# Level 32 of a blockwise triangular inverse: pairs of 32x32 tiles in different row and column groups of TensorE

## The reference

```python
def step(state, inp):
    q_t, k_t, v_t, b_t, g_t = inp
    state = state * jnp.exp(g_t)[..., None, None]
    for j in range(nh):
        kj = k_t[:, j]
        corr = jnp.einsum('bhk,bhkv->bhv', kj, state)
        u = (v_t[:, j] - corr) * b_t[:, j][..., None]
        state = state + jnp.einsum('bhk,bhv->bhkv', kj, u)
    o_t = jnp.einsum('bhk,bhkv->bhv', q_t, state)
    return (state, o_t)
```

## Time and profile before

| | us |
|---|---|
| median of 3 runs | 1023.55 |
| runs | 1021.53, 1023.55, 1026.05 |
| profiled execution, its own time | 1018.88 |
| its span | 1016.9 |
| PE busy | 884.0 |
| DVE, ACT, POOL busy | 526.5, 388.9, 335.1 |
| mean granted clock of TensorE | 0.93 of 2.4 GHz |

### The profile page before, as it was taken

How to read it: one execution, slowest core, us unless ns; L and a number is a source line. 1 busy time by engine, 2 the same in 40 slices (tenths; PEclk the granted TensorE clock), 3 DMA queues, 4 the chain that set the end, 5 groups by cost and what they waited for, 6 DMA issues and landing times.

```text
span 1016.9 us, 15663 instructions
## 1 busy us (share of the span) xinstructions
PE 884.0 (87%) x5306; PEld 629.4 (62%) x5307; DVE 526.5 (52%) x1233; ACT 388.9 (38%) x834; POOL 335.1 (33%) x648
## 2 busy tenths in 40 slices
PE   6586889999999999999999984871699999999993
PEld 3334466686766766766766874661466666666662
DVE  1377756867868768768778641345541111111113
ACT  2453746446456445545554420202222222222220
POOL 0105853547358357346454471000041000000005
PEclk9797979999999999999999995975599999999997
DMA  7303013102120130031021011009717100000104
GB/s 208 104 0 68 2 20 74 22 12 63 22 50 25 22 73 15 8 74 22 2 43 21 12 26 26 1 1 328 247 52 273 55 31 31 31 31 31 31 16 124
DMA packets 100623, 58.39 MB, mean 57 GB/s; under 512 B 62088, under 2 KB 95952, under 8 KB 100560
## 3 DMA queue, kind: packets, MB, share of 16 engines
q1 hardware_dynamic: 99024, 53.38, 19.4%
q0 software_dynamic: 1536, 4.20, 1.4%
HBM read 43.00 MB, written 14.55 MB: 57 GB/s over the span
## 4 chain that ended last, share of the span: by engine, by line
PE 71%; DVE 8%; ACT 5%; POOL 5%; issue 5%; DMA 4%; SPq 1%; ACTq 0%; DVEq 0%; POOLq 0%
PE bank L1480 15%; PE bank L524 10%; PE bank L1526 8%; PE bank L605 3%; PE bank L673 3%; DVE y L934 3%; PE bank L650 3%; PE bank L532 3%; POOL inv L1225 2%; POOL term L1222 2%; PE bank L635 2%; PE bank L581 2%; PE bank L654 2%; PE bank L649 2%; PE bank L1511 2%
## 5 line engine op out<-in xcount | busy, mean ns | idle before, releaser
L934 DVE SCALAR_TENSOR_TENSOR y<-bank,cwh,y 128x510 f32<-128x510 f32 (+2 forms) x240 | 177.6, 744 | 68.4 <-ACT y L745 64.6
L524 PE MATMUL bank<-xnT,wbuf 128*128 128x512 f32 x320 | 162.0, 631 | 7.5 <-DVE y L934 7.0
L1480 PE MATMUL bank<-f_wgu,f_xgT 128*128 x368 | 118.8, 466 | 0.0
L1222 POOL TENSOR_TENSOR term<-inv,blk 128x126 f32<-128x126 f32 (+22 forms) x248 | 87.4, 353 | 57.8 <-DMA blk<-a_blocks 39.0
L1734 DVE TENSOR_TENSOR f_act<-f_sg,bank 128x352 f32<-128x352 f32 x62 | 32.2, 521 | 142.0 <-PE bank L1480 140.0
L524 PEld LDWEIGHTS bank<-xnT,wbuf 128*128 128x128 f32 x320 | 56.2, 195 | 69.6 <-issue 53.4
L1225 POOL TENSOR_TENSOR inv<-inv,term 128x126 f32<-128x126 f32 (+22 forms) x248 | 91.2, 368 | 19.4
L1526 PE MATMUL bank<-f_wdn,f_actT 128*128 (+1 forms) x372 | 91.5, 387 | 0.8 <-ACT f_actT L1596 0.8
L1805 POOL DMA_INDIRECT f_back<-slots_y,f_slot x16 | 15.4, 960 | 228.1 <-DMA slots_y<-f_yb 221.5
L1583 ACT ACTIVATE f_sg<-bank 128x352 f32<-128x352 f32 x62 | 28.8, 464 | 160.8 <-PE bank L1480 160.8
L1480 PEld LDWEIGHTS bank<-f_wgu,f_xgT 128*128 128x128 f32 x368 | 66.2, 190 | 36.8 <-issue 7.6
(11 more groups left out here) (211 smaller groups left out, 1604.7 us busy)
## 6 DMA issues: line engine op xcount, KB each, us to landing
f_wgu<-in_exp_gu SPq DMA_DIRECT2D x8, 1408.0 KB, 8.9
f_wdn<-in_exp_dn SPq DMA_DIRECT2D x8, 640.0 KB, 9.7
blk<-a_blocks SPq DMA_DIRECT2D x16, 256.0 KB, 3.8
slots_x<-oT SPq DMA_DIRECT2D x24, 128.0 KB, 1.8
f_xg<-slots_x SPq DMA_DIRECT2D x24, 128.0 KB, 2.0
slots_y<-f_yb SPq DMA_DIRECT2D x23, 128.0 KB, 1.7
wbuf<-in_Wk SPq DMA_DIRECT2D x16, 128.0 KB, 3.6
wbuf<-in_Wv SPq DMA_DIRECT2D x16, 128.0 KB, 3.5
```

The lines of the kernel that those rows point to most:

```text
L524: last = mm(bankA[p % 2][:, :], wbuf[A.par][:, kt, wblk, :], xnT[:, kt, (p % 2) * 512:(p % 2 + 1) * 512], start=kt == 0, stop=kt == 1)
L934: v.scalar_tensor_tensor(out=y[p % 2][:, :, k:], in0=src[:, :, 0:SEQ - k], scalar=cwh[A.par][:, cb, 3 - k:4 - k], in1=y[p % 2][:, :, k:], ...
L1222: g.tensor_tensor(step_term, inv[:, 0:r, j:j + 1].to_broadcast([P, r, k]), blk[:, j:j + 1, j + 1:].to_broadcast([P, r, k]), ALU.mult).then ...
L1480: last = mm(gu[c][:, 0:FFH], xt[:, k, :], wgu[:, e, k, at:at + FFH], start=k == 0, stop=k == 1)
```

## The change

Each matmul of p32 and of t32 becomes two of 32x32, one for each pair of blocks (g = 0, 1). For p32 the weights are the 32x32 block of A in rows 0 to 31 (g = 0) or 64 to 95 (g = 1), and the result goes to partitions 32 to 63 or 96 to 127; for t32 the rows are 32 to 63 or 96 to 127 and the result goes to partitions 0 to 31 or 64 to 95. The row group of the array follows from the operands' partitions, the column group from the result's, so the two of a pair use different row groups and different column groups. Both write the same bank. The matmuls are issued in the order chunk 0 g 0, chunk 0 g 1, chunk 1 g 0, and so on. X1 needs only 32 columns, nothing has to be zero any more, the memsets and their semaphore go, and the copies read packed columns.

```diff
-    X1 = sb("X1", [P, BC, STEPS])
+    X1 = sb("X1", [P, BC, NB])
@@ tensor_program, item
                 if kind == "p32":
-                    last = mm(bank[:, cols], a_m, X1[:, m, :], start=True, stop=True)
+                    for g in range(2):
+                        src, out = slice(2 * g * NB, (2 * g + 1) * NB), slice((2 * g + 1) * NB, (2 * g + 2) * NB)
+                        last = mm(bank[out, k * NB:(k + 1) * NB], a_m[src, out], X1[src, m, :], start=True, stop=True)
                 elif kind == "t32":
-                    last = mm(bank[0:32, cols], P32[:, m, :], t_m.rearrange("p (g s c) -> p g s c", s=2, c=32)[:, :, 1, :], start=True, stop=True)
+                    for g in range(2):
+                        src, out = slice((2 * g + 1) * NB, (2 * g + 2) * NB), slice(2 * g * NB, (2 * g + 1) * NB)
+                        last = mm(bank[out, k * NB:(k + 1) * NB], P32[src, m, :], t_m[src, src], start=True, stop=True)
@@ scalar_program, item
+            tiles32 = bank[:, 0:BC // 2 * NB].rearrange("p (m c) -> p m c", c=NB)
             if kind == "p32":
-                if B.h == 0:
-                    act.wait_ge(zeros_done, 1)
-                a(P32[32:64, ms, :], full[32:64, :, 0:32], ACT.Copy)
-                a(P32[96:128, ms, :], full[96:128, :, 32:64], ACT.Copy).then_inc(p32_done, 1)
+                a(P32[32:64, ms, :], tiles32[32:64, :, :], ACT.Copy)
+                a(P32[96:128, ms, :], tiles32[96:128, :, :], ACT.Copy).then_inc(p32_done, 1)
             elif kind == "t32":
-                a(tt[0:32, ms, 32:64], full[0:32, :, 0:32], ACT.Copy)
-                a(tt[64:96, ms, 96:128], full[0:32, :, 32:64], ACT.Copy).then_inc(t32_done, 1)
+                a(tt[0:32, ms, 32:64], tiles32[0:32, :, :], ACT.Copy)
+                a(tt[64:96, ms, 96:128], tiles32[64:96, :, :], ACT.Copy).then_inc(t32_done, 1)
@@ vector_program, turn_blocks
-            if B.h == 0:
-                dve.wait_ge(zeros_done, 1)
-            else:
+            if B.h:
                 item_done(dve, "p32", B.h - 1, 1)
...
-                v.transpose(X1[rows_, :, g * NB:(g + 1) * NB], tt[rows_, :, rows_]).then_inc(x1_done, 1)
+                v.transpose(X1[rows_, :, :], tt[rows_, :, rows_]).then_inc(x1_done, 1)
@@ gpsimd_program
-        g.memset(X1[:, :, :], 0.0)
-        g.memset(P32[:, :, :], 0.0).then_inc(zeros_done, 1)
```

More of the change, by code:

```diff
@@ L303, in attention @@
     tt_zero = sem("tt_zero")
-    zeros_done = sem("zeros_done")
     a_out = sem("a_out")
```

## The result

| | kernel before | changed kernel |
|---|---|---|
| median | 1023.92 us (4 runs) | 997.67 us (4 runs) |
| runs | 1021.53 to 1026.05 | 991.33 to 1000.65 |
| profiled execution | 1018.88, span 1016.9 | 998.55, span 996.6 |
| PE busy | 884.0 | 858.3 |

The ratio is 0.9736, 95% interval 0.9684 to 0.9789. Two later series of the same kernel gave 0.9771 (0.9722 to 0.9820) and 0.9741 (0.9704 to 0.9778). The change is worth 2.3 to 2.7%, 24 to 27 us, where 11 were forecast. The predicted range of 996 to 1022 holds the median, but by its mechanism this is rival 1, and the forecast's own range, 1008 to 1018, was missed. The profiled execution of before, 1018.88 us, is not among the four and was faster than each of them.

The account below looks back on a forecast made before the run. It took TensorE (PE), 87% busy, to bound the kernel. Savings of 8.5 us in the six steady heads and 2.6 in heads 0 and 7, 11.1 in all, off the median 1023.55 gave 1012 us, range 996 to 1022.

Parts of the forecast that it names:

- rival 1: p32 and t32: the two tiles overlap fully, 14.5 ns a pass, 3.27 us saved a steady head, total 999; 25%.
- What bounds the kernel: Whole kernel: PE, busy 87% of the span, carries 71% of the last chain, so p32's saving arrives at the end.
- The price of a pass: p32 and t32 in 32x32 tiles: 29 ns a pass, 64 passes each, net 1.41 us saved per steady head (1 to 6).
- the low end: p32 and t32: 14.5 ns a pass, half of L498's 29, if the tiles overlap as fully and nothing else binds.
- the prediction's own sign: p32 and t32: the forecast is wrong if passes are not at 25 to 33 ns, whatever the total says.
- The 0.20 us for changes of shape: Around p32 in each steady head: one gap of about 0.10 us ahead and one behind.
- Heads 0 and 7: p32 and t32 at half clock: 58 ns a pass, clock rising at the same moment, together 2.6 us saved.
- What is late next: Behind the shorter p32: L649 needs U, smallest margin 0.7 us in head 1; nothing changes on X1's way.
- Rival 2: p32 and t32: passes of long runs come no closer than 56 ns, total 1040; decides from 40 ns on; 10%.
- rival 3: p32 and t32: the two row groups take turns in one bank, 0.10 us each change of tile, total 1062; 4%.
- Rival 4: Each head: PE arrives earlier and waits, 1.4 us of new waits, no change, 1021 to 1025; 10%.
- Rival 5: Steady heads: the clock falls since little of the array works, about 4.5 us lost in each, total 1040; 3%.

Follow-up runs that it names:

- full2: The changed kernel run again unaltered, with a later profile: 994.62 us for 1023.17 of the kernel before (0.9741).
- micro: Changed kernel with nine series of 32 small matmuls ahead of its work, one execution: 32.0 ns a pass for one 32x32 tile, 16.0 for two.
- grouped: Changed kernel with all eight chunks of g = 0 issued first, then all of g = 1: 1020.62 us, 0.9954 of the kernel before.
- again: The changed kernel run once more unaltered: 1001.82 us for 1026.69 of the kernel before (0.9771).
- mixed2: Changed kernel with t32 of heads 0 and 7 as one matmul per chunk, as before: 992.80 us against 994.62 for the changed kernel unaltered.
- warm2: Changed kernel with 8 and 18 full matmuls on old data while PE waits for X1 in heads 0 and 7: 990.69 us against 994.62 unaltered.

## Why the prediction was wrong

- What bounds the kernel, and that the saving in steady heads reaches the end: right for five of the six. 3.06 us of items, 3.08 us of the way from head to head. Of head 6's saving only 1.0 us (2.0 in full2) arrives at p32 of head 7, which waits for X1; the prediction held that nothing changes on X1's way.
- The price of a pass: wrong, and this is the step that failed. The terms "64 x 0.029" of p32 and t32 measured 64 x 0.016. The prediction took its number from L498 and from the case of tiles that don't overlap, and saw in their agreement a confirmation; but L498's 29 ns were two 64-column tiles side by side, and a 64x64 tile alone takes 59 (micro). The same overlap on 32 columns gives half of 32. The text had this as the low end, 14.5 ns, from the same row, and gave it 25%. micro, grouped and the trace agree that it is 16 when tiles take turns and 27 to 32 when they don't. By the prediction's own sign, passes outside 25 to 33 ns, it is wrong, whatever the total says.
- The floor of about 25 ns from start to start that it cites from the Trainium skill ("TensorE: Matmul & The Clock Gate", "Wait — 56ns, not 53.3ns?") did not hold either: the 64 matmul records of a kind start 16.0 ns apart in the mean, and 8.9 with four tiles.
- The 0.20 us for changes of shape: right, 0.22.
- Heads 0 and 7: the sum was 2.6 us, the profile 2.7 (3.5 in full2), by two errors, so the agreement is luck. The passes were half as dear as assumed, and the clock did not rise at the moment it had before: after 12.4 and 16.1 us of work instead of 10.4 and 8.9. In head 7 this took all of the gain up to t64. In head 0 the later rise is in the first profile only; again and full2 have 10.4 and 10.7.
- What is late next: the wait for U in head 1 was named, and shows (0.2 us). Two waits that it left out count for more: that for aT ahead of L577, which takes 0.5 of t32's 0.78 us once p32 is small, and that for X1 in head 7.
- Rival 1 had the items nearly right. Its 1.13 us for p32 counts the gap ahead of it too, and so does 1.24 measured; t32 was 1.03 said and 1.13 measured; 3.27 us a steady head said, 3.06 measured. Its total of 999 stands against 997.67, but that is in part luck: the 3.4 to 3.6 us gained behind t64 are in no sum. Rival 2 (40 ns and more a pass) and rival 3 (row groups take turns in the bank) did not happen, and micro excludes them for these shapes. Rival 4 (new waits take the gain) did not happen either.
- Rival 5, the clock, does not occur in the steady heads of the changed kernel, but it does in grouped, and in head 7 the clock stays down longer.

Open: how much the longer half-clock stretch of head 7 costs in the mean. In the times the runs differ by 2 to 4 us in the expected direction (mixed2 and warm2 against full2), less than their scatter; in the profiles half clock behind p32 of head 7 costs the full change 5 to 8 us and the kernel before 6, so as far as so few profiles can tell, the change adds little to it. What in a run of small tiles keeps the clock down was not taken apart further, nor why it stays up near the end of the attention in the full change and not in the kernel before. The fastest version run is warm2, 990.69 us, and it is not told apart from the full change.

## What to carry to other kernels

Two small fp32 matmuls (32x32 and 64x64 here) in different row or column groups take the time of one, if they are issued by turns; in blocks one after the other they overlap only where the tile changes. So compare what a tile costs alone with what a row in the trace shows, and ask first whether that row was one tile or two. Small tiles right behind idle time can keep the clock low longer than the large ones they replace, so look at the granted clock behind each long wait before the saving is counted there. And divide the gain of a pair of profiles by stretches from marker to marker: a total that fits can hold gains and losses that the change didn't make.

## What was not expected of the hardware

- An fp32 pass of a 32x32 tile costs 32.0 ns alone, 16.0 with two tiles, 8.9 with four; 8 streamed columns cost as much as 32.
- Column groups alone overlap as fully as row groups (16.0 each), and two row groups that write other partitions of the same bank do too.
- The clock fell to 0.50 with no idle time in the 7 us before it, behind 64 passes of one 32x32 tile at a time (grouped, at 210 and 285 us). In head 0 of grouped it stayed at 0.50 for 24 us of unbroken work.
